# Quantising and turning the feed-forward weights inside two earlier stages, and handing them on through memory

## What is computed

```python
def fp4_quant_dequant(x):                      # blocks of 16 along the last dim
    scale = jnp.maximum(jnp.max(jnp.abs(xb), axis=-1, keepdims=True) / 6.0, 1e-12)
    idx = jnp.searchsorted(_MID, jnp.abs(xb / scale))
    return _GRID[idx] * jnp.sign(xb) * scale   # _GRID 0, .5, 1, 1.5, 2, 3, 4, 6
def fp4_linear(x, w):
    return jnp.einsum('bsk,nk->bsn', fp4_quant_dequant(x), fp4_quant_dequant(w))
gate, y = fp4_linear(x, w_gate), fp4_linear(x, w_up)     # w_gate, w_up: 704 x 256
out = fp4_linear(silu(gate) * y, w_down)                 # w_down: 256 x 704
...
h = relu(einsum('nd,edf->enf', x, W1) + b1)              # the experts, for chosen rows only
y = einsum('enf,efd->end', h, W2) + b2
```

## Time and profile before

| what | value |
|---|---|
| median of 3 runs | 3755.53 us (3752.97 to 3761.95) |
| profiled execution, its own time | 3763.9 us |
| its span in the trace | 3762.2 us |
| mean granted clock of TensorE | 0.923 |
| busy in the span: PE, DVE, ACT, Pool | 3245.0, 2918.1, 2060.2, 1191.6 us |

### The profile page before, as it was taken

One profiled execution on the slowest core, in us unless ns is written; L12 is line 12 of the kernel. 1 busy time (PEld: TensorE's weight loads), 2 busy tenths in 40 slices (PEclk: granted clock), 3 DMA queues, 4 the chain that ended last, 5 costly groups with the idle time before them and its releaser, 6 DMA issues. The chain is left out here.

```text
span 3762.2 us, 87543 instructions
## 1 busy us (share of the span) xinstructions
PE 3245.0 (86%) x34874; PEld 1864.2 (50%) x34875; DVE 2918.1 (78%) x4552; ACT 2060.2 (55%) x2972; POOL 1191.6 (32%) x917
## 2 busy tenths in 40 slices
PE   4769999999999999984899776996999999657876
PEld 1433333333333333343566452342778787546665
DVE  5658999999999999925444254775899999758986
ACT  0215777777777777762011155665674765235553
POOL 0310000000000000006000460000999999747775
PEclk8877999999999999996899867998999999879998
DMA  1574031230303030044222253334444434311110
GB/s 56 201 213 48 5 49 19 36 49 5 49 6 49 5 49 6 5 132 170 66 64 65 90 162 107 132 120 139 133 132 121 132 113 134 93 45 51 56 34 17
DMA packets 222017, 297.04 MB, mean 79 GB/s; under 512 B 56393, under 2 KB 155089, under 8 KB 219985
## 3 DMA queue, kind: packets, MB, share of 16 engines
q1 hardware_dynamic: 210944, 268.86, 26.5%
q0 software_dynamic: 6144, 17.05, 1.4%
q10 hardware_dynamic: 4576, 6.13, 0.5%
HBM read 174.88 MB, written 116.47 MB: 77 GB/s over the span
## 5 line engine op out<-in xcount | busy, mean ns | idle before, releaser
L930 DVE TENSOR_REDUCE att_maxima<-att_ps_m 128x1 f32<-128x512 f32 x2048 | 1285.7, 686 | 81.0 <-PE att_ps_m L986 79.4
L885 ACT ACTIVATE att_probs<-att_ps_s 128x1024 f32<-128x1024 f32 x1024 | 1000.6, 1023 | 281.0 <-PE att_ps_o L1013 268.3
L1013 PE MATMUL att_ps_o<-att_probs,att_vs 128*32 128x256 f32 x8192 | 658.3, 393 | 4.8 <-ACT att_probs L885 0.6
L986 PE MATMUL att_ps_m<-att_ks,att_qs 48*128 48x512 f32 x2048 | 585.1, 512 | 29.5 <-DMA att_ks<-scratch_k 28.9
L2252 POOL TENSOR_TENSOR ss_ch<-ss_h,ss_c_rep 128x1024 f32<-128x1024 f32 x256 | 601.8, 2411 | 8.0 <-DVE ss_h L2339 7.9
L2371 PE MATMUL ss_ps_u<-ss_diag,ss_dx_t 128*32 128x128 f32 x16384 | 476.2, 275 | 26.5 <-DMA ss_dx_t<-scratch_dx_t 14.4
L2371 PEld LDWEIGHTS ss_ps_u<-ss_diag,ss_dx_t 128*32 128x32 f32 x16384 | 455.3, 111 | 82.6 <-issue 65.9
L986 PEld LDWEIGHTS att_ps_m<-att_ks,att_qs 48*128 48x128 f32 x2048 | 238.6, 188 | 473.3 <-DVE att_maxima L930 391.3
L1001 PE MATMUL att_ps_s<-att_qs,att_ks 50*128 50x512 f32 x2048 | 454.3, 405 | 2.8 <-ACT att_probs L885 1.4
L2291 ACT ACTIVATE ss_decay<-ss_delta,ss_a_neg 128x1024 f32<-128x1024 f32 x256 | 294.6, 1151 | 227.4 <-DVE ss_h L2339 204.9
L1013 PEld LDWEIGHTS att_ps_o<-att_probs,att_vs 128*32 128x32 f32 x8192 | 162.6, 108 | 361.4 <-issue 340.2
(11 more groups left out here) (389 smaller groups left out, 4522.5 us busy)
## 6 DMA issues: line engine op xcount, KB each, us to landing
ss_delta<-scratch_delta SPq DMA_DIRECT2D x256, 128.0 KB, 3.3
att_qs<-scratch_q SPq DMA_DIRECT2D x96, 128.0 KB, 6.9
att_ks<-scratch_k SPq DMA_DIRECT2D x96, 128.0 KB, 8.7
ex_x<-scratch_sorted_x SPq DMA_DIRECT2D x72, 132.0 KB, 2.1
scratch_sorted_y<-ex_y SPq DMA_DIRECT2D x72, 128.0 KB
scratch_v<-qkv_v_ext SPq DMA_DIRECT2D x8, 1024.0 KB, 4.4
scratch_q<-qkv_parts SPq DMA_DIRECT2D x16, 512.0 KB, 5.3
scratch_k<-qkv_parts SPq DMA_DIRECT2D x16, 512.0 KB, 6.0
```

Source lines behind the costliest of these rows:

```text
L885: act.activation(probs[:, (2 * n + pair) % 4, :, :], ps_s[pair][:, :, :], ACT.Exp, scale=HD ** -0.5).then_inc(exp_done, 1)
L930: dve.tensor_reduce(maxima[:, j, at:at + 1], ps_m[plan.bank(key)][:, :], AX.X, ALU.max).then_inc(maxed, 1)
L986: pe.matmul(ps_m[plan.bank(key)][:, :], qs[own, s // QC % 2, s % QC, p, t * P:(t + 1) * P], ks[own, s // QC % 2, p, c * GN:(c + 1) * GN], ...
L1013: mm = pe.matmul(ps_o[h * VW:(h + 1) * VW, cols], vs[st // QC % 2][:, kt, h * VW:(h + 1) * VW], probs[:, (2 * n + h // 2) % 4, h % 2, cols ...
```

## The change

The block `fp4_weights` is gone. What it did is spread over three places.

- In `experts` ACT issues the five loads of the weights before its own work. DVE gets a fourth stage, `quantise`, five steps behind: in 72 half steps it rounds 36 slices of 128 columns (`SLICE`); even half steps find the scales and divide, odd ones round. Pool finishes each slice (`scale_slice`). DVE waits at the end for the last slice.
- In `moe_output` PE turns the weights by the same 36 transposes (14 batches, three of them in flight) before it waits for `loaded`, ACT copies, DVE takes the low halves, and ACT stores the results in three transfers to memory (`scratch.gate_up_t`, twice 1.44 MB, and `scratch.down_t`, 0.79 MB), before it waits for `loaded`.
- In `fp4_ffn` SP's `load_first` reads them back, behind the loads of units 0 and 1; PE waits for them before the first `gate_up`.

```diff
 class Routing:
+        self.ffn = room.sb("ffn", [P, FFN_COLS])          # SLICE = 2 * FFN_COLS // SORTED = 128
...
 def experts
             @block.scalar
                 act.sem_inc(y_taken, 2)
+                for w, name in enumerate(("w_gate", "w_up")):
+                    act.dma_start(gate_up[:, w, :HT - 1, :], ...).then_inc(ffn_loaded, 16)
+                    act.dma_start(gate_up[:FFN_LAST, w, HT - 1, :], ...).then_inc(ffn_loaded, 16)
+                act.dma_start(down[:, :, :FFN], ...).then_inc(ffn_loaded, 16)
+            @block.gpsimd
+                def scale_slice(n, slot):
+                    pool.wait_ge(fp4_rounded, n + 1)
+                    pool.tensor_tensor(rounded[:, :], rounded[:, :], magic[:, :], ALU.subtract).then_inc(less_magic, 1)
+                    pool.wait_ge(less_magic, n + 1)
+                    pool.tensor_tensor(in_blocks(raw[:, bass.ds(n * SLICE, SLICE)]), in_blocks(rounded[:, :]),
+                                       over(fp4_by[:, :].unsqueeze(2), [P, SLICE // FP4, FP4]), ALU.mult).then_inc(quantised, 1)
+                run_stages(pool, SORTED // 2, (scale_slice, 0))
             @block.vector
+                def quantise(m, slot):
+                    n2 = m - slot
+                    if isinstance(m, int) and m == 0:
+                        dve.wait_ge(ffn_loaded, 5 * 16)
+                        dve.wait_ge(padded, 2)
+                    if slot == 0:
+                        if not isinstance(m, int) or m > 0:
+                            dve.wait_ge(quantised, n2 // 2)
+                        fp4_scale(dve, c, x, amax[:, :], fp4_by[:, :], inverse[:, :])
+                        c.then(dve.tensor_tensor(q, x, over(inverse[:, :].unsqueeze(2), ...), ALU.mult))
+                        c.wait()
+                        return
+                    fp4_nearest(dve, c, f, q).then_inc(fp4_rounded, 1)
-                run_stages(dve, SORTED, (scale_x, 0), (add_b1, 1), (clip_hidden, 2))
+                run_stages(dve, SORTED, (scale_x, 0), (add_b1, 1), (clip_hidden, 2), (quantise, 5))
+                dve.wait_ge(quantised, SORTED // 2)
...
 def moe_output
+        def turn_room(n):
+            return (ps_w[:, :], ps_x[:, 0, :], ps_x[:, 1, :])[n % 3]
             @block.vector
+                for n, (_, dst, width) in enumerate(turned_weights()):
+                    if n < SPLITS:
+                        dve.wait_ge(wt_copied, n + 1)
+                        split_low(dve, dst[1], turn_room(n)[:, :width], dst[0]).then_inc(wt_split, 1)
             @block.scalar
+                for n, (_, dst, width) in enumerate(turned_weights()):
+                    act.wait_ge(wt_turned, n + 1)
+                    act.activation(dst[0], turn_room(n)[:, :width], ACT.Copy).then_inc(wt_copied, 1)
+                act.wait_ge(wt_split, SPLITS)
+                for half in range(2):
+                    act.dma_start(scratch.gate_up_t[half], ...).then_inc(wt_stored, 16)
+                act.wait_ge(wt_copied, TURNS)
+                act.dma_start(scratch.down_t, ...).then_inc(wt_stored, 16)
                 act.wait_ge(loaded, 5 * 16)
             @block.tensor
+                for n, (tiles, _, _) in enumerate(turned_weights()):
+                    if n >= 3:
+                        ...  # waits for wt_split or wt_copied of batch n - 3
+                    for i, tile in enumerate(tiles):
+                        mm = pe.transpose(turn_room(n)[:, i * P:(i + 1) * P], tile, ident[:, :])
+                    mm.then_inc(wt_turned, 1)
                 pe.wait_ge(loaded, 5 * 16)
...
+def fp4_nearest(dve, c, magic, rounded):           # the last three steps of fp4_round, by themselves
...
-def fp4_weights(nc, io, ident, gate_up_t, down_t, load_first):
...
 def fp4_ffn
             for u in range(2):
                 load(sp, u, u)
-        fp4_weights(nc, io, ident, gate_up_t, down_t, load_first)
+            for half in range(2):
+                sp.dma_start(gate_up_t[half][:, :, :]..., scratch.gate_up_t[half]).then_inc(ffn_loaded, 16)
+            sp.dma_start(down_t[:, :, :]..., scratch.down_t).then_inc(ffn_loaded, 16)
             @block.sync
+                load_first(sp)
                 def gate_up(u, slot, k):
+                    if isinstance(u, int) and u == 0:
+                        pe.wait_ge(ffn_loaded, 3 * 16)
```

More of the change, by code:

```diff
@@ L1069, in _ @@
                 turn_out(STEPS - 1)
+FP4 = 16
+FFN = 704
+HT = -(-FFN // P)
+HEAD, REST = GN, FFN - GN
+GU_COLS, DOWN_COLS = 2 * HT * C, KC * HT * P
+FFN_COLS = GU_COLS + DOWN_COLS
+FFN_LAST = FFN - (HT - 1) * P
+SLICE = 2 * FFN_COLS // SORTED
 class Routing:
@@ L1434, in experts @@
         w1, w2, b1 = route.w1, route.w2, route.b1
+        raw = route.ffn
+        magic, rounded = (r.sb(n, [P, SLICE]) for n in ("magic", "rounded"))
+        amax, fp4_by, inverse = (r.sb(n, [P, SLICE // FP4]) for n in ("amax", "fp4_by", "inverse"))
+        ffn_loaded, padded, fp4_steps, fp4_rounded, less_magic, quantised = (
+            r.sem(n) for n in ("ffn_loaded", "padded", "fp4_steps", "fp4_rounded", "less_magic", "quantised"))
         ps_x = [r.ps(f"ps_x{i}", [P, KC, GN // 2]) for i in range(2)]
@@ L1476, in _ @@
                 run_stages(act, SORTED, (take_y, 3), ways=WAYS)
+            @block.gpsimd
+            def _(pool):
+                gate_up = raw[:, :GU_COLS].rearrange("p (w t c) -> p w t c", w=2, t=HT)
+                down = raw[:, GU_COLS:].rearrange("p (k f) -> p k f", k=KC)
+                pool.memset(gate_up[FFN_LAST:, :, HT - 1, :], 0.0).then_inc(padded, 1)
+                pool.wait_ge(padded, 1)
+                pool.memset(down[:, :, FFN:], 0.0).then_inc(padded, 1)
+                def scale_slice(n, slot):
[5 more added lines that the diff above has]
+                run_stages(pool, SORTED // 2, (scale_slice, 0))
             @block.vector
@@ L1574, in moe_output, with turned_weights @@
         ps_b = [r.ps(f"ps_b{i}", [P, GT, C]) for i in range(2)]
+        gate_up_t = [r.sb(f"gate_up_t_{half}", [P, KC, 2 * FFN], F32R) for half in ("high", "low")]
+        down_t = r.sb("down_t", [P, HT, C])
+        ps_w = r.ps("ps_w", [P, GN])
+        wt_turned, wt_copied, wt_split, wt_stored = (r.sem(n) for n in ("wt_turned", "wt_copied", "wt_split", "wt_stored"))
+        def turned_weights():
+            gate_up = route.ffn[:, :GU_COLS].rearrange("p (w t c) -> p w t c", w=2, t=HT)
+            down = route.ffn[:, GU_COLS:].rearrange("p (k f) -> p k f", k=KC)
+            for w in range(2):
+                for k in range(KC):
+                    src = [gate_up[:, w, t, k * P:(k + 1) * P] for t in range(HT)]
+                    yield src[:HEAD // P], [half[:, k, w * HEAD:(w + 1) * HEAD] for half in gate_up_t], HEAD
+                    at = 2 * HEAD + w * REST
+                    yield src[HEAD // P:], [half[:, k, at:at + REST] for half in gate_up_t], REST
+            for f in range(HT):
+                yield [down[:, k, f * P:(f + 1) * P] for k in range(KC)], [down_t[:, f, :]], C
+        SPLITS, TURNS = 4 * KC, 4 * KC + HT
+        def turn_room(n):
+            return (ps_w[:, :], ps_x[:, 0, :], ps_x[:, 1, :])[n % 3]
         loaded = r.sem("loaded")
@@ L1753, in turn_xn @@
                 def turn_xn(g, slot):
+                    if g == 0:
+                        pe.wait_ge(wt_copied, TURNS)
                     pe.wait_ge(xn_normed, (g + 1) * GT)
@@ L2430, in fp4_round @@
     c.wait()
+    return fp4_nearest(dve, c, magic, rounded)
+def fp4_nearest(dve, c, magic, rounded):
     c.then(dve.tensor_scalar(magic.bitcast(I32), rounded.bitcast(I32), 0x7F800000, None, ALU.bitwise_and))
@@ L2581, in fp4_ffn @@
         gated, xm, x2 = r.sb("gated", [P, 2, DT, UT * P]), r.sb("xm", [P, 2, UT, C]), r.sb("x2", [P, 2, UT, C])
-        w_loaded, in_loaded = r.sem("w_loaded"), [r.sem(f"in_loaded{i}") for i in range(2)]
+        w_loaded, ffn_loaded, in_loaded = r.sem("w_loaded"), r.sem("ffn_loaded"), [r.sem(f"in_loaded{i}") for i in range(2)]
         def unit_rows(ap, u):
@@ L2595, in load_first @@
                 load(sp, u, u)
-        fp4_weights(nc, io, ident, gate_up_t, down_t, load_first)
+            for half in range(2):
+                sp.dma_start(gate_up_t[half][:, :, :].rearrange("p k f -> p (k f)").bitcast(F32), scratch.gate_up_t[half]).then_inc(ffn_loaded, 16)
+            sp.dma_start(down_t[:, :, :].rearrange("p h c -> p (h c)"), scratch.down_t).then_inc(ffn_loaded, 16)
         y, z = r.sb("y", [P, UT, C]), r.sb("z", [P, UT, C])
```

113 lines of the change are left out of this document (19 added, 94 removed).

## The result

The changed kernel took 3723.8 us in the median (3720.3 to 3726.6, four executions) against 3758.7 for the kernel before beside it: a ratio of 0.9896, interval 0.987 to 0.9922. It is faster, and 3.8 us from the forecast of 3720, 3.2 of which are the kernel before, which I had put at 3755.53. Two later comparisons, on other occasions, gave less: 0.9931 (0.9907 to 0.9954) and 0.9929 (0.9911 to 0.9948). The medians differed by 35.0, 28.4 and 27.0 us, some 30 on average. The three intervals overlap (29 to 49, 17 to 35 and 20 to 33 us), so they don't contradict each other. The rest of this document is about those 5.

The account below looks back on a forecast made before the run. It took a 51 us chain between scan and feed-forward stage, with no engine near full, to lie wholly on the critical path. −38.7 + 1 + 1 + 1 = −35.7 us from the profiled 3763.9, median-adjusted, gave 3720 us (range 3710 to 3735).

Parts of the forecast that it names:

- Feed-forward stage, 41.0 less the clock's 2.3: Feed-forward stage: first `project` starts 41.0 us sooner (40.0 to 41.4); its half-rate clock gives 2.3 back (0 to 4.7).
- 38.7: Feed-forward stage: sum of its terms, 38.7 us less.
- The reload: Feed-forward stage: unit 2's reload, queued behind the turned weights, costs 0 us (0 to 5.1 against).
- Experts' loop, 0: Experts' steady loop: a slice's 1.05 us a step fits VectorE's 2.08 us of waits, costing 0 us.
- The 0.67 a step: Experts' loop: VectorE slows beside Pool by 0.67 us a step, making 1.7 of 2.08 us.
- Experts' start, +1 (0 to 3): Experts' start: ScalarE's 2.16 MB of weight loads beside the first units' rows cost 1 us (0 to 3).
- Experts' tail, +1: Experts' end: last half steps and Pool's last slice take 6.9 us plus barrier against 6.7, costing 1 us (0 to 3).
- Sums, +1 (−4 to +6.3): Sums: turning hides under the wait for gathers; stores beside the last gathers cost 1 us (−4 to +6.3).
- the rival: Sums: the stores' long rows starve the gathers, which land last, +6.3 us instead of +1: 3725 us; chance 15%.
- the −4 end of my range: Sums: turning might hold up the clock, so 8 us of first `bias` would take 4.
- 35.7: Whole kernel: −38.7 + 1 + 1 + 1 = −35.7 us.
- The slower rival: Experts' loop: VectorE becomes the bound past 2.08 us a half step, each microsecond above costing 72; at 2.75, 3768; chance 4%.

Follow-up runs that it names:

- the added stores: Kernel before the change plus three ScalarE stores (3.67 MB, data nobody reads) behind the first group's gates copy in the sums: 3744.9 us against 3742.8.
- the trace with 3632 packets: Changed kernel with the turned weights' copy in memory laid out in rows of 1,024 bytes, not 11,264: 3714.9 us against 3714.4 unchanged.
- the combined kernel: Changed kernel with later weight loads, quantising two steps sooner, stores at group 6, 45 turnings before first `bias`, 34 before first `project`: 3727.4 us against 3731.2.

## Why the prediction came out right, step by step

**Feed-forward stage, 41.0 less the clock's 2.3: right.** The first `project` moved by 49.60 − 8.11 = 41.5 us, `project` took 6.29, and the first `gate_up` moved by 75.24 − 36.34 = 38.9 us, where 38.7 stood. The reload cost nothing, as taken: it was issued 14.3 us behind the last weights' load. The stage as a whole gave 35.2 us in the first pair and 35 to 42 over all executions, 38.9 in the mean of ten. The spread has a term that the forecast did not have. The part behind the first `gate_up`, where the change has no instruction, took 414.5 to 415.3 us in six of these ten traces and 418.9 to 419.3 in four, the first among them; before it took 415.6, and 414.1 with the added stores. The four are those whose first `project` took 6.2 to 6.3 us (5.1 to 5.6 in the six), and in the 40 us behind the first `gate_up` their granted clock was 0.83, where it was 0.91 in the six and before. So in four of ten the clock cost 4 us more. Whether the change brings this about stays open, with only two traces of the old block.

**Experts' loop, 0: right.** Even half step 0.28 + 0.17 + 0.20 + 0.29 = 0.94 us (1.0 forecast), odd 0.22 + 0.23 + 0.29 = 0.74 (0.75). One part was under-priced: behind an even half step VectorE stands [0.59 <-DVE ex_rounded], so the even one costs 1.6 with its gaps, not 1.2. No slowing beside Pool is seen: the scaling of the rows, the only work of VectorE that runs beside Pool's two instructions here, keeps its 0.73 us. Where the two engines did hold each other up was the sums. The 0.67 a step of the forecast was not spent.

**Experts' start, +1 (0 to 3): wrong, +3.2 to +4.0.** The failing step is "only the first two units are waited for at once (0.27 MB, 0.7 us at full rate)". It took the rows as if they went first. ScalarE's first load was issued 0.8 us ahead of SyncE's, and both share one set of engines, which was full: 349 to 353 GB/s from 1794 to 1802. Two units wait, one after the other, behind the 2.16 MB.

**Experts' tail, +1: right**, 4.22 against 3.17 us, and for the reason given.

**Sums, +1 (−4 to +6.3): the rival happened at its place.** The turning went better than forecast: the stores were issued at 2111.1 to 2113.1 instead of by 2117. That put them squarely on the gathers, and these landed 4.0 us later. My "If shared fairly, 0.13 MB more of gathers cost under 1 us" is the sentence that failed: by then the stores met six of the eight gathers and not two. The reason given for the rival isn't borne out either. On the rule of the Trainium skill (DMA: Bandwidth & Descriptors, "Queues, rings and completion order"), that the engines take turns between queues by packets, I had taken a row for a packet. By it, read so, the gathers should have gained from rows of equal length, and the trace with 3632 packets against 432 shows 6.91 us against 6.64. Whether the 4 us reach the end of the stage stays open: the stage scatters by 16 us, the kernels with added stores and with all edits differ from their partners in the three slow additions as well, and Pool's gather of group 2 waits for `bias`, whose length for one group went from 10.9 to 16.3 us with the clock.

**The clock's part.** The first trace's −3.4 us for the sums looked like the −4 end of my range, the turning holding up the clock. But in that trace the clock was 1.00 behind the turning (2111 to 2115) and 0.50 again when `bias` began (2117 to 2127). Seven more executions of the same code, five of them near 187 us, show that the −3.4 was chance.

**Sum.** With the places as measured: −38.9 (to −40.9) + 3.2 to 4.0 + 1.05 + about 4 for the gathers gives −29.8 to −32.7 (without the gathers' 4, −34 to −37). That leaves out the clock behind `gate_up`; with the feed-forward stage's mean of ten, −38.9, and 3.6 at the start it is −30.2. The three comparisons average −30. The first comparison's −35.0 met the forecast, with a start that cost 2 to 3 us more than taken and gathers that cost 3 more. That it came within 1 us of 35.7 was luck: in its pair of traces 6.4 us came from untouched stages and from a short execution of the sums. The range of 3710 to 3735 came from the bounds and held.

**The slower rival** had the right mechanism. Its slope has one measured point: 2.40 us added where 1.44 to 1.47 were free gave +32.1 us, 0.93 to 0.96 of the excess for each of the 36 pairs. Its own point was put too far out: the waits overstate the room, here by 0.46 us of 1.9 in a pair of steps, so it lies at 1.85 us for a half step and not at 2.08 (4.16 − 0.46 = 3.70 for two). With 1.44 us left it was far enough away all the same.

## What to carry to other kernels

Work that fits into an engine's waits cost nothing here until the room was used up, and then nearly all of the excess; the room is less than the waits of a steady step add up to (1.44 of 1.9 us here), since part of each is a gap that stays. What comes with the work, its loads and stores, was the dearer part: megabytes issued beside small transfers that someone waits for delayed these by 3 to 4 us in both stages, with long rows and with short, and moving the issue (behind the first units, or to group 6) took the delay away. In a stage that scatters by 16 us, judge an edit by the place that it moves and not by one execution's total; and look at single instructions that got longer, since a delay can bring two engines together that didn't meet before.

## What was unexpected of the hardware

The same code of one stage took 178 to 194 us with a mean granted clock of 0.72 to 0.66. In it, VectorE's addition of 1024 columns took 3.6 to 4.1 us in place of 1.23 whenever Pool's product began during it, though the addition had begun first; one that met only the end of the product took 1.35. TensorE's instructions can come late without any wait: in the kernel with 70 added turnings gaps of 0.3 to 1.4 us, all put down to "issue", ran from 2120.9 to 2133.7, and in the combined kernel two of 0.5 and 1.1 us from 2130.5; in twelve traces without turnings ahead of `bias` there is none over 0.3 us from 10 to 43 us into the stage. What causes them wasn't settled. And a store split into 1 KB rows takes its issuing engine longer: for the 768 KB of `down_t` ScalarE spent 3.83 us in place of 1.02.
